# The second expert layer: gathers three experts ahead, inverse roots taken while the tokens are chosen, weights loaded there, and a down projection with 512 tokens moving

## The reference, cut to what matters

```python
scores = jax.nn.softmax(xf @ gate_w.T, axis=-1)
vals, idx = jax.lax.top_k(scores.T, k)            # n = 8 experts, k = 512 tokens each
y = xf[flat_idx].reshape(k, n, d)
y = (y - mu) * jax.lax.rsqrt(var + LN_EPS) * ln_w + ln_b
h = jax.nn.gelu(jnp.einsum('knd,nfd->knf', y, fc1s) + b1s, approximate=True)
out = (jnp.einsum('knf,ndf->knd', h, fc2s) + b2s) * kept_w[..., None]
xf = xf.at[flat_idx].add(out.reshape(k * n, d))
```

## Time and profile before

| what | us |
|---|---|
| median of 3 runs | 830.31 (830.15 to 830.43) |
| the profiled execution's own time | 829.71 |
| its span | 828.0 |
| `choose1`, from its first instruction to the end | 598 to 657 |
| `experts1` | 657 to 806.5 |
| `finish` | 806.5 to 828 |

### The profile page before, as it was taken

One profiled execution on the slowest core, in us unless ns is written; L12 is line 12 of the kernel. 1 busy time (PEld: TensorE's weight loads), 2 busy tenths in 40 slices (PEclk: granted clock), 3 DMA queues, 4 the chain that ended last, 5 costly groups with the idle time before them and its releaser, 6 DMA issues. The chain is left out here.

```text
span 828.0 us, 16573 instructions
## 1 busy us (share of the span) xinstructions
PE 577.7 (70%) x5632; PEld 391.7 (47%) x5633; DVE 465.2 (56%) x1216; ACT 321.6 (39%) x685; POOL 405.4 (49%) x661
## 2 busy tenths in 40 slices
PE   2769788888888753899928888888411359878910
PEld 1335445445545332899915566656200236555610
DVE  1646666755766326455516899999587622222105
ACT  1035655565556720355514556564300021312105
POOL 7034544544454520544256588863240156777623
PEclk9978989988999955899967999999855556978665
DMA  4674656655530000222221111210100113434217
GB/s 115 139 172 91 144 117 124 125 111 109 108 70 16 15 13 1 58 67 70 55 65 39 40 53 52 68 44 28 51 8 0 41 44 58 86 62 87 23 16 203
DMA packets 72935, 57.69 MB, mean 70 GB/s; under 512 B 15608, under 2 KB 62624, under 8 KB 72864
## 3 DMA queue, kind: packets, MB, share of 16 engines
q1 hardware_dynamic: 64928, 47.72, 24.8%
q0 software_dynamic: 7936, 9.05, 6.3%
HBM read 36.95 MB, written 19.53 MB: 68 GB/s over the span
## 5 line engine op out<-in xcount | busy, mean ns | idle before, releaser
L578 DVE TENSOR_REDUCE a_mx<-a_psR 128x6 f32<-128x768 f32 x128 | 121.8, 954 | 65.6 <-PE a_psR L316 63.9
L245 POOL TENSOR_SCALAR_AFFINE_SELECT a_pr<-a_pr 128x512 f32<-128x512 f32 x128 | 81.3, 635 | 134.8 <-ACT a_pr L492 134.7
L492 ACT ACTIVATE a_pr<-a_psR 128x768 f32<-128x768 f32 x128 | 103.5, 810 | 86.6 <-PE a_psR L329 85.8
L756 POOL DMA_INDIRECT e_xt<-x1d,source x40 | 38.1, 952 | 54.9 <-PE e_psX L767 33.4
L1642 POOL DMA_INDIRECT acc<-e_ot,e_ixa x32 | 50.3, 1572 | 23.3 <-DVE e_ot L1682 11.8
L308 PE MATMUL a_psR<-a_maskA,identb 128*128 128x256 bf16 x256 | 54.0, 296 | 8.6 <-DMA a_ks<-qkd 8.0
L336 PE MATMUL a_psO<-a_pr,a_va 128*32 128x256 f32 x512 | 46.9, 442 | 3.8 <-ACT a_onT L484 2.1
L1707 ACT ACTIVATE e_hT<-e_psH,e_b 128x512 f32<-128x512 f32 x32 | 22.0, 687 | 70.6 <-PE e_psH L1727 69.4
L1743 PE MATMUL e_psY<-e_w,e_hT 128*128 128x128 f32 x256 | 46.6, 338 | 1.9 <-ACT e_hT L1707 1.9
L326 PE MATMUL a_psR<-a_qs,a_ks 50*128 50x256 bf16 x256 | 37.6, 291 | 14.2 <-DMA a_qs<-a_mlo 11.5
L1007 POOL TENSOR_TENSOR a_rs<-a_ve,mhalf 128x2 f32<-128x2 f32 x32 | 22.8, 711 | 47.9 <-DVE a_ve L1255 46.8
(11 more groups left out here) (296 smaller groups left out, 1434.0 us busy)
## 6 DMA issues: line engine op xcount, KB each, us to landing
qkd<-a_hml SPq DMA_DIRECT2D x16, 384.0 KB, 3.0
e_w<-in_fc SPq DMA_DIRECT2D x16, 256.0 KB
a_qs<-qkd SPq DMA_DIRECT2D x32, 96.0 KB
a_ks<-qkd SPq DMA_DIRECT2D x32, 96.0 KB
ys<-e_yt SPq DMA_DIRECT2D x40, 64.0 KB, 1.5
a_qs<-qkd SPq DMA_DIRECT2D x32, 64.0 KB
a_ks<-qkd SPq DMA_DIRECT2D x32, 64.0 KB
x1d<-a_x SPq DMA_DIRECT2D x16, 128.0 KB, 1.8
```

What stands on the lines that cost most here:

```text
L245: g.affine_select(out=diagonal, in_=diagonal, pattern=[[0, 4], [1, 128]], compare_op=ALU.is_ge, fill=0.0, base=0, channel_multiplier=-1).t ...
L492: a.activation(pr[s][:, :, 0:3, :].rearrange("p x k q -> p x (k q)"), psR[:, r:r + 2, 0:384], ACT.Exp).then_inc(probs, 1)
L578: v.tensor_reduce(mx[b % 2][:, :, 2 * u:2 * u + 35:17], psR[:, r:r + 2, 0:384].rearrange("p x (k c) -> p x k c", c=128), AX.X, ALU.max).th ...
L756: pool.indirect_dma_start(xt[n % 4][:], None, x1d, bass.IndirectOffsetOnAxis(ap=source[:, n:n + 1], axis=0)).then_inc(x_in[n % 4], 16)
```

## The change

The change touches the last three stages before `finish`.

- `attention1` keeps the mean, variance and inverse root of every token in `moments` and `roots` instead of in tiles that are overwritten. Its instructions are the same.
- `choose1`: SP first issues the loads of all eight experts' weights, 16 DMAs of 256 KB, into the tiles that held the first expert layer's weights. POOL, after its constants, computes a root for each token, (var * root^2 + eps)^-0.5, which normalises a row whose mean is zero, and half the score; both go to `tab` in one DMA, whose rows are now 137 values (548 bytes).
- `experts1`: four small loads in front. POOL takes the indices straight from `ids`, has no copies and no root, and issues the gathers of experts 0, 1 and 2, then for each expert e the gather of e + 3 and the add of e. DVE has one instruction for the normalised rows and one for the output, each 128 x 512 with a broadcast factor. PE keeps the weights stationary in the down projection and moves 512 tokens, four matrix multiplications, ACT adds the bias on the way to SBUF (`dT`), and PE transposes the result back, four transposes. All is written out, without the loop.

```diff
@@ attention1
-                    scale_and_shift(ve3, mv3, rs3, nr3, r3_step, X, rstd3)
+                    scale_and_shift(ve3[:], moments[:, 2 * X:2 * X + 2, :], roots[:, 2 * X:2 * X + 2, :], nr3[:], r3_step, X, rstd3)
...
@@ choose1, sync
-            sp.wait_ge(p_sb, 1)
-            sp.dma_start(scored.rearrange("(t p) e -> p t e", p=128), pb[:]).then_inc(pb_out, 16)
+            for e in range(E8):
+                sp.dma_start(w1[:, e], fc1T[e]).then_inc(w_in, 16)
+                sp.dma_start(w2[:, e], fc2T[e]).then_inc(w_in, 16)
+            sp.wait_ge(rows_sb, 1)
+            sp.dma_start(scored.rearrange("(t p) e -> p t e", p=128), rows[:]).then_inc(pb_out, 16)
@@ choose1, gpsimd, behind L1419
+            g.tensor_tensor(var[:], A["roots"][:], A["roots"][:], ALU.mult).then_inc(var_sb, 1)
+            pool.wait_ge(var_sb, 1)
+            g.tensor_tensor(var[:], var[:], A["moments"][:, :, 1:2], ALU.mult).then_inc(var_sb, 1)
+            pool.wait_ge(var_sb, 2)
+            g.tensor_scalar(var[:], var[:], EPS, None, ALU.add).then_inc(var_sb, 1)
+            pool.wait_ge(var_sb, 3)
+            g.tensor_tensor(rows[:, :, E8:], var[:], A["mhalf"][:, 0:1, :].broadcast_to([128, NT, 1]), ALU.pow)
+            pool.wait_ge(p_sb, 1)
+            g.tensor_scalar(rows[:, :, 0:E8], pb[:], 0.5, None, ALU.mult).then_inc(rows_sb, 1)
@@ experts1, sync: all that it loads
+            for dst, src in ((lw[:], lnw), (lb[:], lnb), (b1[:], b1c.rearrange("e p c -> p e c")), (b2[:], b2c)):
+                sp.dma_start(dst, src).then_inc(c_in, 16)
@@ experts1, gpsimd, in place of L1611 to L1648
+            def gather(e):
+                if e >= RING:
+                    pool.wait_ge(o_sb, e - RING + 1)
                 for a in range(C):
+                    pool.indirect_dma_start(xg[e % RING][:, a, :], None, tab, bass.IndirectOffsetOnAxis(
+                        ap=ids[:, C * e + a:C * e + a + 1], axis=0)).then_inc(x_in[e % RING], 16)
+            def scatter(e):
+                pool.wait_ge(o_sb, e + 1)
+                if e >= 1:
+                    pool.wait_ge(added, 16 * C * e)
+                for a in range(C):
+                    pool.indirect_dma_start(acc, bass.IndirectOffsetOnAxis(ap=ids[:, C * e + a:C * e + a + 1], axis=0),
+                                            ot[e % 2][:, a, :], None, compute_op=ALU.add).then_inc(added, 16)
+            for e in range(AHEAD):
+                gather(e)
+            for e in range(E8):
+                if e + AHEAD < E8:
+                    gather(e + AHEAD)
+                scatter(e)
+            pool.wait_ge(added, 16 * C * E8)
@@ experts1, vector, in place of L1654 to L1692
+            def normed(e):
+                dve.wait_ge(x_in[e % RING], 16 * C * (e // RING + 1))
+                if e >= 2:
+                    dve.wait_ge(x_ps, e - 1)
+                x = xg[e % RING]
+                v.tensor_tensor(yn[e % 2][:], x[:, :, 0:D], x[:, :, R - 1:R].broadcast_to([128, C, D]), ALU.mult
+                                ).then_inc(yn_sb, 1)
+            def weighted(e):
+                dve.wait_ge(z_ps, e + 1)
+                if e >= 2:
+                    dve.wait_ge(added, 16 * C * (e - 1))
+                v.tensor_tensor(ot[e % 2][:], psZ[e % 2][:].rearrange("p (a d) -> p a d", d=D),
+                                xg[e % RING][:, :, D + e:D + e + 1].broadcast_to([128, C, D]), ALU.mult).then_inc(o_sb, 1)
+            normed(0)
+            for e in range(E8):
+                if e + 1 < E8:
+                    normed(e + 1)
+                weighted(e)
@@ experts1, scalar
+            transposed(0)
+            for e in range(E8):
+                for c in range(4):
+                    act.wait_ge(h_ps, 4 * e + c + 1)
...
+                    a_.activation(hT[e % 2][:, c, :], psH[c][:], ACT.Gelu_apprx_tanh, bias=b1[:, e, c:c + 1]).then_inc(h_sb, 1)
+                if e + 1 < E8:
+                    transposed(e + 1)
+                act.wait_ge(d_ps, e + 1)
+                if e >= 2:
+                    act.wait_ge(z_ps, e - 1)
+                a_.activation(dT[e % 2][:], psD[:], ACT.Identity, bias=b2[:, e:e + 1]).then_inc(dT_sb, 1)
@@ experts1, tensor
+            def down(e):
+                if e >= 1:
+                    pe.wait_ge(dT_sb, e)
+                for c in range(4):
+                    pe.wait_ge(h_sb, 4 * e + c + 1)
+                    last = mm(psD[:], w2[:, e, c, :], hT[e % 2][:, c, :], start=(c == 0), stop=(c == 3))
+                last.then_inc(d_ps, 1)
+            def transpose_out(e):
+                pe.wait_ge(dT_sb, e + 1)
+                if e >= 2:
+                    pe.wait_ge(o_sb, e - 1)
+                for a in range(C):
+                    last = nc.tensor.transpose(psZ[e % 2][:, 128 * a:128 * a + 128], dT[e % 2][:, 128 * a:128 * a + 128],
+                                               A["ident"][:])
+                last.then_inc(z_ps, 1)
+            pe.wait_ge(w_in, 32 * E8)
+            transpose_in(0)
+            up(0)
+            for e in range(E8):
+                if e + 1 < E8:
+                    transpose_in(e + 1)
+                down(e)
+                if e + 1 < E8:
+                    up(e + 1)
+                transpose_out(e)
```

More of the change, by code:

```diff
@@ L1313, with choose1 @@
 F1 = 4 * D
-def choose1(nc, A, logits, scored, ids):
+def choose1(nc, A, logits, scored, ids, w1, w2, fc1T, fc2T, w_in):
     ctx = ExitStack()
@@ L1339, in choose1 @@
         pb = sb("pb", full)
+        rows = sb("rows", [128, NT, E8 + 1])
+        var = sb("var", [128, NT, 1])
         byx = sb("byx", [128, 2, E8, SEG])
@@ L1583, in experts1 @@
-        block = ctx.enter_context(nc.Block())
-        def iterations(eng, body, last=True):
-            body(None, Seq(0, 0))
-            body(Seq(0, 0), Seq(0, 1))
-            body(Seq(0, 1), Seq(0, 2))
-            with eng.Fori(1, E8 // 2 - 1) as j:
-                for k in range(2):
-                    body(Seq(j, k), Seq(j, k + 1))
-            body(Seq(0, E8 - 2), Seq(0, E8 - 1))
-            body(Seq(0, E8 - 1), None)
+        psX, psH, psD = psum("psX"), [psum(f"psH{c}") for c in range(4)], psum("psD")
@@ L1625, in body @@
-            def body(s, n, g):
-                if n:
-                    pool.wait_ge(var, n.n + 1)
-                    nc.gpsimd.tensor_tensor(rs[:], ve[:], A["mhalf"][:, 0:C], ALU.pow).then_inc(rstd, 1)
-                if g:
-                    gather(g)
-                if s:
-                    if later(s):
-                        pool.wait_ge(added[s.p], 16 * C * s.half)
-                    nc.gpsimd.tensor_copy(ixa[s.p][:], ids[:, bass.ds(C * s.n, C)]).then_inc(ixa_sb, 1)
-                    pool.wait_ge(ixa_sb, s.n + 1)
-                    pool.wait_ge(o_sb, s.n + 1)
-                    if later(s, 1):
-                        before = Seq(0, s.n - 1)
-                        pool.wait_ge(added[before.p], 16 * C * (before.half + 1))
-                    hold(A, pool)
-                    for a in range(C):
-                        pool.indirect_dma_start(acc, bass.IndirectOffsetOnAxis(ap=ixa[s.p][:, a:a + 1], axis=0),
-                                                ot[s.p][:, a, :], None, compute_op=ALU.add).then_inc(added[s.p], 16)
@@ L1686, in _ @@
-            for i in range(-2, 2):
-                body(Seq(0, i) if i >= 0 else None, Seq(0, i + 2))
-            with dve.Fori(1, E8 // 2 - 1) as j:
-                for k in range(2):
-                    body(Seq(j, k), Seq(j, k + 2))
-            for i in (E8 - 2, E8 - 1):
-                body(Seq(0, i), None)
+            def normed(e):
[5 more added lines that the diff above has]
+                                ).then_inc(yn_sb, 1)
@@ L1746, in _, with transpose_in, up @@
-            iterations(pe, body)
+            def transpose_in(e):
+                pe.wait_ge(yn_sb, e + 1)
+                if e >= 1:
+                    pe.wait_ge(yT_sb, e)
+                for a in range(C):
+                    last = nc.tensor.transpose(psX[:, 128 * a:128 * a + 128], yn[e % 2][:, a, :], A["ident"][:])
+                last.then_inc(x_ps, 1)
+            def up(e):
+                pe.wait_ge(yT_sb, e + 1)
+                for c in range(4):
+                    if e >= 1:
+                        pe.wait_ge(h_sb, 4 * (e - 1) + c + 1)
+                    mm(psH[c][:], w1[:, e, 128 * c:128 * c + 128], yT[e % 2][:], start=True, stop=True).then_inc(h_ps, 1)
@@ L1859, in build @@
         attention1(nc, A, x1d, ys, slot, qkv1, b1col, b1row, off, lin2, lin2b, gate, tab[:, 0:D], acc, logits)
-        choose1(nc, A, logits, tab[:, D:D + E8], ids)
-        experts1(nc, A, tab, acc, ids, fc1, b1s, fc2, b2s, lnw, lnb)
+        choose1(nc, A, logits, tab[:, D:], ids, fcs, pjs, fc1, fc2, late)
+        experts1(nc, A, tab, acc, ids, fcs, pjs, late, b1s, b2s, lnw, lnb)
         finish(nc, A, acc, out)
```

167 lines of the change are left out of this document (37 added, 130 removed).

## The result

The changed kernel takes 800.83 us in the median of 4 runs (798.4 to 802.13), the kernel before 830.23 us beside it (827.54 to 830.43). The ratio is 0.9659, with a 95% interval from 0.9625 to 0.9694: 3.4% faster. The forecast was 802.0, the range 797 to 811. The profiled execution took 800.24 us with a span of 798.5 us, against 829.71 and 828.0 before.

A forecast was written before the change was run, and what follows sets the result against it. The prediction took POOL's pace to bound the middle of the second experts. From 829.7 us it took 15.5 for pace and 12.8 for the start, giving 801.4, plus 0.6 for the median: 802.0 us, range 797 to 811.

The forecast's parts named there:

- The sum: Whole kernel: 829.7 less 15.5 and 12.8 gives 801.4 us for the profiled execution, 802.0 for the median.
- end unchanged: Last expert's adds to `finish`: 14.8 us in all, which nothing in the change touches.
- Pace on POOL: Second experts, add 0 to add 7: four cycles of 12.8 and three of 9.8 us, 15.5 us less.
- gone are the root and both copies: POOL, each cycle with gathers: 2.5 us less, from 15.3 to 12.8 us per expert.
- POOL keeps its pauses: Rival, chance 0.10: the pause before each group of indirect DMAs stays, 5.5 us lost, 807.5 us.
- Landing waits: Adds 5, 6 and 7, without gathers in front, wait for earlier adds to land: 9.8 us each (9.4 to 10.1).
- The start: Second experts up to the first add: first add at 682.8 against 695.60, 12.8 us less.
- The clock: PE at the start of the second experts: half clock rises to full 4.8 us into up, at 672.0.
- The rival built on it: Chance 0.03: PE at half clock through all second experts becomes the bound, last adds 7.2 us later, 837.5 us.
- The prediction's own reading: PE in the second experts: clock stayed half with 128-column instructions; the new 512-column down has the form that restores it.
- Moved into the choosing: Weight loads and table's new columns in `choose1`: both end before 640, the DVE chain at 657, so cost 0.

The follow-up runs named there:

- u_down: Old down projection (128-column matmuls, bias as a fifth matmul, no transposes back) put back into the changed kernel: 798.87 us, ratio 0.9687.
- u_roots: Statistics and root put back in each expert of the changed kernel, with DVE's old order: 808.55 us, ratio 0.9794.
- n_fix20: n_spread with one order mended: PE and ACT turn back expert 6's output before touching expert 7's input: 788.31 us, ratio 0.9590.
- u_rootq: u_roots with each root moved in front of the next expert's gathers on POOL, as in the kernel before: 813.59 us, ratio 0.9835.
- n_spread: Changed kernel with 20 gathers before the first add, twelve spread between adds, a buffer per input, DVE reordered: 800.68 us, ratio 0.9686.
- c_after: The changed kernel measured again with no edit: 799.68 us, ratio 0.9681.
- u_hold: Only hold()'s semaphore instruction put back before each group of indirect DMAs on POOL in the changed kernel: 801.72 us, ratio 0.9689.
- n_ahead4: Changed kernel with one more group of gathers ahead (AHEAD = 4): 802.33 us, ratio 0.9706.

## Why the prediction was right, and where it was not

**The sum.** 80.6 us from add 0 to add 7 against 80.5 measured; first add at 682.8 against 681.48, which is 683.0 when the 1.5 us of scatter ahead of the stage are put back; end unchanged (0.3 less). 802.0 against 800.83. The forecast adds up the steps of the changed kernel, so it held without knowing all that the old one spent; what it names as saved is in part wrong.

**Pace on POOL.** The bound was the right one for the changed kernel, and for four of the seven cycles of the kernel before. POOL issues without a gap through the first five groups, and PE's 14 us of extra work in u_down or gathers one group earlier do not change what a cycle costs. 12.8 and 9.8 us were forecast, 12.9 and 9.65 measured. The step "gone are the root and both copies" had the right size (2.5, measured 15.3 - 12.9 = 2.4) and a wrong owner. The copies cost 0.1 us a cycle (13.0), copy and `hold()` together 1.2 more (14.2), and the root the remaining 1.1, by difference (0.75 when it is put back alone, without the pauses behind it; all three together were not put back). The diff took out `hold()` in the same lines, and the prediction never priced it. It read a pause behind a copy as the copy's. The rival "POOL keeps its pauses" is dead: the pauses are neither the copy's nor any group's.

The 15.6 us are 9.6 in the four cycles with gathers and 6.0 in the three without, which took 11.5, 10.6 and 12.8 us before and 9.7, 9.6 and 9.6 now. The prediction never took those three apart and put the whole difference down to POOL's pace. In the kernel before POOL waits there for an output each time, the last one in the earlier trace rows:

```profile
763.47 1.64 POOL L1628 TENSOR_TENSOR e_rs<-e_ve,mhalf 128x4 f32<-128x4 f32 x1
...
766.40 1.12 DVE L1682 TENSOR_SCALAR e_ot<-e_psY,e_gate 128x128 f32<-128x128 f32 x4
...
768.31 1.61 POOL L1642 DMA_INDIRECT acc<-e_ot,e_ixa  x1 [3.06 <-DVE e_ot L1682]
...
778.95 1.57 POOL L1642 DMA_INDIRECT acc<-e_ot,e_ixa  x1 [3.30 <-DVE e_ot L1682]
```

The root of expert 7 stands behind the adds of expert 4 on POOL, though its variance is ready at 759.0. DVE makes the input of 7 ahead of the output of 5, which PE had ready at 759.8. PE idles 3.14 us for that input, its clock falls, and down of expert 6 takes 10.0 us in place of 6.0, up of expert 7 6.0 in place of 3.7. u_roots has the first part of this: its three cycles are 10.3, 9.8 and 9.6, 0.8 us of the 6.0. The other 5.2 us no kernel brings back, since none has both the roots and the old down projection. By the rows above I estimate 4 us of them for the half clock: with 6.0 and 3.7 us the last two groups of adds would have waited for landings alone.

**Landing waits.** 9.8 was put together from the end of the kernel before and came out at 9.65, of which 2.5 is the wait seen alone. The Trainium skill, "DMA: Bandwidth & Descriptors", section "Rules for kernel authors", says that an accumulating DMA needs a wait for the earlier one's semaphore where both touch the same bytes. By that the wait can't go, and no run here tried; it can be covered. n_fix20 puts two gathers (2.5 us) into three of the gaps, and there the next group begins 0.30 us behind them.

**The start.** 12.8 forecast, 12.2 and 0.4 measured. The sum of forward steps through the changed kernel was good: 24.9 us from first gather to first add against 25.1. About 1 us of the agreement is luck, for the measured start holds 1.0 us of a late `dT` (last section) that no step had. What the old start was made of was not seen: it ran over POOL's queue, not over PE. u_roots and u_rootq divide the 12.2 us. Statistics and root on the way of expert 0 cost 4.2, where 3.3 were counted. The root of an expert in front of the next gathers cost 3.8, and nobody had priced it. The other 4.2 are mostly the copies and pauses of four groups and the late rows of expert 2 (u_rootq). The wide down projection, which the steps counted as 3.5 in place of 6.0 us, brought nothing: its transposes back wait behind up of expert 1 on PE.

**The clock.** It rose some 4.7 us into up (the eight take 5.96 us where 3.6 is full), as taken. In the changed kernel it fell once, in the longest idle time (4.6 us, at 718 to 722), and came back inside the next down projection. Granted clock by stretch, in the columns of the earlier trace rows:

```profile
718.00:722.00 4.00, 0.00 (x0) 0.00 (x0) 0.87 (x2) 0.15 (x1) 3.39 (x3) 0.94 0.23 53
723.00:728.00 5.00, 5.00 (x9) 2.40 (x8) 0.00 (x0) 0.78 (x1) 4.08 (x4) 0.50 0.36 34
729.00:733.00 4.00, 4.00 (x13) 1.80 (x12) 0.00 (x0) 2.84 (x5) 2.86 (x4) 1.00 0.23 53
```

Down took 6.06 us there in place of 3.6, and POOL did not notice. Four idle times of 1.4 us and one of 1.9 left it at full. The Trainium skill's rule that idle gaps between bursts put the clock back to half ("TensorE: Matmul & The Clock Gate", section "Why this matters for your kernels") agrees with the trace for the long gap. In the kernel before one of 2.03 us ended at half clock and one of 2.56 us (in front of 720.73) at full, so the length of a gap alone doesn't tell. The rival built on it needed a cold PE in every expert, and behind the start that was so in one. The prediction's own reading, that 128-column instructions keep the clock down and 512-column ones bring it back, is half borne out. In the kernel before three down projections ran to their end at half clock, and it came back in the up phase behind them; with the wide form it came back within one down or up phase wherever it fell (the changed kernel, u_roots, n_fix20), at the latest 6.9 us into it (n_spread). But in u_down the 128-column form ran at full clock behind the start, where PE had no idle time over 1.2 us. By these runs the form matters for coming back, not for staying up.

**Moved into the choosing.** Cost 0 as forecast: the chain takes 58.0 us before and after. The root of 32 elements took 5.5 us (bound 13), the loads were issued by 606, the table's columns landed by 625 (bound 640).

## What to carry to other kernels

Find the queue that never waits, and price what stands in it instruction by instruction, the semaphore ones too; a pause behind an instruction is not that instruction's until it has been taken out alone. Work that is in order on a queue holds back everything behind it: a root in front of a gather, the transposes of a late input in front of a ready output. When a queue is the bound, put its free instructions where it waits for landings and for the first result; the same 64 DMAs in another order were worth 8 us, as much as all statistics and roots in u_roots. And a difference that comes out right is not yet a cause: take apart what the old kernel spent there, too.

## What the runs showed of the hardware that was not expected

- A semaphore instruction on POOL costs nothing in front of an indirect DMA (0.30 us from the DMA ahead, with it or without), and a wait for POOL's own copy costs nothing either (0.27). One behind the other they cost 0.57 us more (0.84).
- ACT and DVE start some instructions up to 4.3 us after all they wait for is done, once, in the first expert: `dT` 22.7 to 22.8 us behind the first gather in the changed kernel, in c_after and in u_hold; down had ended 3.5, 3.6 and 4.0 us before. In n_ahead4 and n_spread it happened four times, the last 28.4 us behind the first gather, which made their starts 4.3 us longer. In n_fix20, with the same 20 gathers as n_spread and a difference only in the code of the last experts, it did not happen; nor in any other of these kernels. The cause is open. The length of the row of gathers alone isn't it. That it depends on where code lies is a guess that nothing here tested. In the changed kernel it costs about 1 us.
- 32 elements a partition to the power -1/2 took 5.48 us on POOL where 4 took 1.04 to 1.63: the price isn't proportional.
